# Scores of a 32-head attention as fp32 products over 16 rows, in four diagonal tiles of TensorE's array

## The reference, cut to what matters

```
x = hidden_states                       # (4, 512, 512) fp32: 2048 tokens of 512
q = (x @ wq.T + bq).reshape(B, S, 32, 16)        # 32 heads of 16
k = (x @ wk.T + bk).reshape(B, S, 32, 16)
v = (x @ wv.T + bv).reshape(B, S, 32, 16)
scores  = einsum('bshd,bstd->bsht', q, k) / 4    # per token: 32 x 32, heads against heads
context = einsum('bsht,bstd->bshd', softmax(scores), v)
x = layernorm(x + context)
dq1, dq2, dq3 = nf4_quant_dequant(w1), nf4_quant_dequant(w2), nf4_quant_dequant(w3)
x = layernorm(x + (silu(x @ dq1.T) * (x @ dq2.T)) @ dq3.T)       # hidden width 1376
```

## Time and profile before

| | |
|---|---|
| median of 3 runs | 787.29 us (787.03 to 789.25) |
| the profiled execution's own time | 788.01 us |
| its span in the profile | 786.2 us |
| busy share of the span | PE 93%, DVE 81%, ACT 62%, POOL 14% |
| mean granted clock of TensorE | 0.862 of full speed |

### The profile page before, as it was taken

The page is one execution under the profiler, slowest core; times in us unless marked ns, Lnnn a source line. Parts: engine busy times, 40 slices in busy tenths (PEclk is TensorE's granted clock), DMA queues, the critical chain, the costliest instruction groups (busy, mean ns, idle before and its releaser), DMA issues.

```text
span 786.2 us, 14305 instructions
## 1 busy us (share of the span) xinstructions
PE 732.7 (93%) x5688; PEld 625.5 (80%) x5688; DVE 633.4 (81%) x876; ACT 484.6 (62%) x650; POOL 106.8 (14%) x101
## 2 busy tenths in 40 slices
PE   4899999966999989999999999999999999999983
PEld 4778788856999989999888877887887788888761
DVE  2699999975888988988888899999977986554386
ACT  3588979773645636546853878877756775333134
POOL 2011012113101101111101121121201111000022
PEclk9999999995555655555799999999999999999995
DMA  9964455999797695995413371211514010330347
GB/s 219 223 182 146 134 166 167 250 305 271 166 261 189 184 283 134 269 216 202 163 26 122 120 230 54 81 39 31 173 59 155 1 61 21 134 119 13 121 147 160
DMA packets 89474, 117.89 MB, mean 150 GB/s; under 512 B 24768, under 2 KB 70848, under 8 KB 86496
## 3 DMA queue, kind: packets, MB, share of 16 engines
q1 hardware_dynamic: 88272, 114.88, 51.6%
q10 hardware_dynamic: 1136, 2.10, 1.2%
HBM read 76.42 MB, written 38.86 MB: 147 GB/s over the span
## 4 chain that ended last, share of the span: by engine, by line
PE 54%; DVE 18%; issue 11%; ACT 8%; DMA 4%; SPq 4%; POOL 1%; DVEq 0%; POOLq 0%; ACTq 0%
PE ps_p L1043 10%; DVE nf_acc L1166 8%; PE ps_s L947 7%; PE ps_s L945 7%; PE ps_s L946 7%; PE ps_p L945 5%; PE ps_p L947 5%; PE ps_p L946 5%; ACT nf_y L777 4%; PE ps_s L1030 3%; PE ps_t L968 2%; DMA qk_parts<-qk_p 2%; DVE part L1298 2%; DMA k_st<-qk_parts 1%; ACT part L852 1%
## 5 line engine op out<-in xcount | busy, mean ns | idle before, releaser
L1166 DVE SCALAR_TENSOR_TENSOR nf_acc<-nf_y,nf_acc 128x1024 f32<-128x1024 f32 (+4 forms) x266 | 298.5, 1122 | 37.6 <-ACT nf_y L777 28.3
L777 ACT ACTIVATE nf_y<-nf_w,bound_b 128x1024 f32<-128x1024 f32 (+4 forms) x285 | 288.9, 1047 | 9.7 <-DVE nf_acc L1162 3.4
L1043 PE MATMUL ps_p<-probT,v_bd 128*68 128x32 f32 x1024 | 125.7, 301 | 7.9 <-issue 7.9
L1043 PEld LDWEIGHTS ps_p<-probT,v_bd 128*68 128x68 f32 x1024 | 122.7, 211 | 9.4 <-issue 8.0
L945 PE MATMUL ps_p<-x_hl,w_hl 128*128 128x512 f32 x192 | 77.6, 404 | 6.1 <-DVE w_hl L1184 4.1
L695 POOL TENSOR_TENSOR nf_w<-nf_w,nf_rec 128x1024 f32<-128x1024 f32 (+4 forms) x19 | 39.5, 2080 | 320.1 <-DVE nf_rec L1150 320.1
L1325 DVE TENSOR_TENSOR silu<-silu,ps_s 128x512 f32<-128x512 f32 (+1 forms) x44 | 30.1, 684 | 61.5 <-PE ps_s L947 61.5
L927 ACT ACTIVATE hid_hl<-silu 128x512 fp32r<-128x512 f32 (+1 forms) x44 | 27.8, 632 | 77.6 <-DVE silu L1325 77.6
L947 PE MATMUL ps_p<-x_hl,w_hl 128*128 128x512 f32 x192 | 75.5, 393 | 0.0
L945 PE MATMUL ps_s<-x_hl,f_ha 128*128 128x512 f32 x192 | 75.4, 393 | 0.0
L946 PE MATMUL ps_p<-x_hl,w_hl 128*128 128x512 f32 x192 | 75.3, 392 | 0.0
(11 more groups left out here) (110 smaller groups left out, 1253.1 us busy)
## 6 DMA issues: line engine op xcount, KB each, us to landing
x_hl<-x_parts SPq DMA_DIRECT2D x10, 2048.0 KB, 8.5
qk_parts<-qk_p SPq DMA_DIRECT2D x64, 204.0 KB, 2.6
q_st<-qk_parts SPq DMA_DIRECT2D x48, 272.0 KB, 6.8
k_st<-qk_parts SPq DMA_DIRECT2D x48, 272.0 KB, 7.2
x_parts<-x_st SPq DMA_DIRECT2D x16, 512.0 KB, 4.4
nf_w<-in_L_ffn_w SPq DMA_DIRECT2D x24, 256.0 KB, 3.0
dequantised<-nf_acc SPq DMA_DIRECT2D x10, 512.0 KB, 2.6
v_blocks<-v_t SPq DMA_DIRECT2D x16, 256.0 KB, 3.5
```

The source lines that it names most:

```text
L777: act.activation(nf_y[0:p, at % NY, 0:w], nf_w[0:p, u % 2, 0:w], ACT.Identity, bias=bound_b[0:p, i:i + 1], scale=STEEP).then_inc(s_ny, 1)
L1043: t = pe.matmul(ps_p[0:MV, (G + 3) % NPV, i * H:(i + 1) * H], v_bd[hb % 2][:, :, g * GI + i], probT[:, G % 2, i], start=True, stop=True)
L1166: dve.scalar_tensor_tensor(out=acc, in0=y, scalar=float(NF4[i + 1]), in1=acc, op0=ALU.min, op1=ALU.max).then_inc(s_nacc, 1)
```

## The change

- **Scores.** q and k are no longer split. They are stored as fp32 and loaded into stacks of the same name with 16 rows in each quarter of the partitions (rows 32q to 32q+15), a quarter of the half block's tokens in each. A product has 16 rows, and its result goes to the quarter of the same number. There are still 64 products for each group, now fp32.
- **Parts.** `part_high`, `part_rest`, `part_middle` and `part_low` give way to one `queries_keys` on ACT. The values' bias moves from ACT to DVE (`value`).
- **Values.** The operands change places: `probT` (128x32) is stationary and `v_bd` (128x68) is moving; the 16 products of a group go to four quarters of the partitions. The result has tokens and heads in rows, so ACT copies it out (`evacuate`, 128x272), PE transposes it back (`back`, four transposes of 128x68), and `context` copies that as before. The rows of `v_bd`, `q_st` and `k_st` are padded from 64 to 68 elements (`VS`).
- **Transfers.** One store for each q or k product instead of two; eight loads for each pair of stacks instead of twelve, and no copies of zero rows. The stacks of half block 1, the values of 0 and the stacks of 0 are loaded in that order during the third and fourth block's projections (`FIRST_LOADS`). `clear(0)` is moved to the start.
- **Order.** `values(G-2)` is before the `ct` turns, `back(G-3)` behind them; contexts, `ct`, `moments`, `norm_1` and `xt` are all one step later, and two `xt` turns fall behind the last step. ACT works a step's levels ahead of its exponential. The levels are dealt out anew: 76 instead of 59 beside the projections, 45 instead of 55 beside the attention steps.
- **Rooms.** The feed-forward tensors lie in another order in SBUF.

```diff
-    Q_TERMS = (0, 1, 2, 0, 1, 0)
-    K_TERMS = (0, 0, 0, 1, 1, 2)
-    TS = TB + 16
+    VS = TI + 4
...
-    qk_d = nc.dram_tensor("qk_parts", [2, NHB, 3 * E, TS], BF16, kind="Internal").ap()
+    qk_d = nc.dram_tensor("queries_keys", [2, NHB, Q4, D, H, VS], F32, kind="Internal").ap()
...
+    FIRST_LOADS = {3 * KC * (NBK - 1) - 5: "stacks 1", 3 * KC * (NBK - 1) - 3: "values 0",
+                   3 * KC * (NBK - 1) + 1: "stacks 0"}
-    LV_P = [1, 1, 1, 1, 1, 1, 1, 1, 2, 2, 2, 2] * NBK
+    LV_P = [2, 1, 2, 1, 2, 1, 2, 1, 2, 2, 2, 2] + [2, 2, 1, 2, 2, 1, 2, 2, 1, 2, 1, 2] * (NBK - 1)
-    LV_A = [2] * GG
+    LV_A = [2, 1] * (GG // 2)
     for b in range(NBK - 1):
-        LV_A[8 * b + 10:8 * b + 13] = [1, 1, 1]
+        LV_A[8 * b + 11:8 * b + 14] = [1, 1, 1]
...
-        def load_stacks(eng, hb, which=range(3), sides=range(2)):
+        def load_stacks(eng, hb):
+            for i in range(2):
+                for q in range(Q4):
+                    eng.dma_start(stacks[hb % 2][i][32 * q:32 * q + D].rearrange("d h t -> d (h t)"),
+                                  qk_d[i, hb, q].rearrange("d h t -> d (h t)")).then_inc((s_ldq, s_ldk)[i][hb % 2], 16)
...
-            def part_high(n):
+            def queries_keys(n):
...
+                act.activation(qk_p[:, n % NQK, :, 0:TI], ps_p[:, tau % 3].rearrange("p (a t) -> p a t", t=TI),
+                               ACT.Identity, bias=bias[:, i, m:m + 1]).then_inc(s_qh, 1)
...
+            def evacuate(G):
+                act.wait_ge(s_pv, G + 1)
+                wait(act, s_back, G - NCT + 1)
+                act.activation(ctmp[:, G % NCT], ps_p[:, G % 2, 0:4 * MV], ACT.Copy).then_inc(s_evac, 1)
...
             for G in range(GG):
+                steep(LV_A[G])
                 for at in CONTEXT_AT.get(G, []):
                     context(at)
-                steep(LV_A[G] // 2)
                 exp(G)
+                if G >= 2:
+                    evacuate(G - 2)
...
                 for i in range(GI):
                     for q in range(Q4):
-                        s = q * TI + g * GI + i
+                        rows, s = slice(32 * q, 32 * q + D), g * GI + i
                         t = pe.matmul(ps_s[32 * q:32 * q + 32, G % 2, i * H:(i + 1) * H],
-                                      q_st[:, :, s], k_st[:, :, s], start=True, stop=True)
+                                      q_st[rows, :, s], k_st[rows, :, s], start=True, stop=True)
...
-                wait(pe, s_ctx, G - NPV + 1)
+                wait(pe, s_evac, G - 1)
                 for i in range(GI):
-                    t = pe.matmul(ps_p[0:MV, (G + 3) % NPV, i * H:(i + 1) * H], v_bd[hb % 2][:, :, g * GI + i],
-                                  probT[:, G % 2, i], start=True, stop=True)
+                    a, j = divmod(i, 4)
+                    t = pe.matmul(ps_p[32 * j:32 * j + 32, G % 2, a * MV:(a + 1) * MV], probT[:, G % 2, i],
+                                  v_bd[hb % 2][:, :, g * GI + i], start=True, stop=True)
                 t.then_inc(s_pv, 1)
+            def back(G):
+                pe.wait_ge(s_evac, G + 1)
+                wait(pe, s_ctx, G - 1)
+                for a in range(4):
+                    t = pe.transpose(ps_p[0:MV, 2 + G % 2, P * a:P * a + P], ctmp[:, G % NCT, a * MV:(a + 1) * MV],
+                                     ident[:])
+                t.then_inc(s_back, 1)
...
-            def part_rest(n):
...
-            def part_low(n):
...
+            def value(n):
...
+                dve.tensor_scalar(v_t[:, n % NV], ps_p[:, tau % 3], bias[:, 2, m:m + 1], None, ALU.add
+                                  ).then_inc(s_vev, 1)
```

More of the change, by code:

```diff
@@ L94, in layer_kernel, with pairs @@
     NU0 = len(GROUPS[0]) + 2
+    def pairs(g):
+        js, out = list(GROUPS[g]), []
+        while js:
+            n = 2 if len(js) > 1 and rows_of(js[1]) == P else 1
+            out.append(js[:n])
+            js = js[n:]
+        return out
     def turns_of(u):
         kind, g, _ = UNITS[u]
-        return [("f", u, s) for s in range(2 if kind == "w" else -(-len(GROUPS[g]) // 2))]
+        return [("f", u, s) for s in range(2 if kind == "w" else len(pairs(g)))]
     def valid(g):
@@ L312, in layer_kernel @@
         s_const = sem("s_const")
-        s_zero = sem("s_zero")
         s_vzero = [sem(f"s_vzero{i}") for i in range(2)]
-        s_szero = [sem(f"s_szero{i}") for i in range(2)]
         s_pad = sem("s_pad")
@@ L396, in parts_stored @@
             for r in range(NQK):
-                wait(eng, s_stq[r], 32 * of_slot(tiles, r, NQK))
+                wait(eng, s_stq[r], 16 * of_slot(tiles, r, NQK))
         def values_stored(eng, tiles):
@@ L733, in ones @@
                 pool.wait_ge(s_vzero[slot], 2 * Q4)
-            words = q_st1[:].rearrange("p h t -> p (h t)").bitcast(F32)
-            for q in range(Q4):
-                pool.memset(words[:, DV * TI * q:DV * TI * q + DV * TI], 0.0).then_inc(s_zero, 1)
             normalise(0)
+            clear(0)
+            ones(0)
             for tau in range(3 * KC * NBK):
-                if tau == VALUES_FREE + 2:
-                    clear(0)
-                    ones(0)
                 around(LV_P[tau])
@@ L902, in _ @@
                     norm_1(NORM_AT[G])
-                steep(LV_A[G] - LV_A[G] // 2)
+            context(GG - 4)
+            evacuate(GG - 2)
+            for key in XT_AT.get(GG, []) + TAIL_1:
+                high(key)
             context(GG - 3)
-            for key in TAIL_1:
-                high(key)
-            context(GG - 2)
             steep(LV_T[0])
@@ L910, in _ @@
                 high(key)
-            context(GG - 1)
+            evacuate(GG - 1)
+            context(GG - 2)
             steep(LV_T[1])
@@ L1104, in _ @@
                 scores(G)
+                if G >= 2:
+                    values(G - 2)
                 for key in CT_AT.get(G, []):
                     turn(key)
-                if G >= 2:
-                    values(G - 2)
+                for at in BACK_AT.get(G, []):
+                    back(at)
                 for key in XT_AT.get(G, []):
@@ L1111, in _ @@
             values(GG - 2)
-            for key in TAIL_1:
+            for key in XT_AT.get(GG, []) + TAIL_1:
                 turn(key)
+            back(GG - 3)
             values(GG - 1)
@@ L1116, in _ @@
                 turn(key)
+            back(GG - 2)
             pe.wait_ge(s_minus_i, 1)
@@ L1120, in _ @@
                 gate_up(s)
+                if s == 0:
+                    back(GG - 1)
                 for key in F_TURNS.get(s, []):
```

201 lines of the change are left out of this document (76 added, 125 removed).

## The result

The changed kernel takes 807.0 us (median of 4 runs, 802.5 to 809.3) against 788.3 for the kernel before in the same comparison: 1.024 times, with an interval of 1.021 to 1.027. It is slower; the forecast was 762, faster. The profiled execution took 808.4 us, span 806.6.

The account below looks back on a forecast made before the run. PE was taken to bind projections, feed-forward and about half the attention steps. Gains of 3.5 + 12.4 + 3.7 - 0.5 = 19.1 us took 788.0 to 768.9; half the clock's gain gave 762, range 740 to 792.

Parts of the forecast that it names:

- PE's step: Attention: PE's work per group falls from 5.15 to 4.41 us, scores 2.56, values 0.97, transposes back 0.88.
- the eight steps of 4.41 and the 144.4 us: Attention: eight opening steps take 35.3 us, 12.4 gained; steps from group 8 to 31 take 144.4, 3.7 gained.
- All this is worth nothing by itself: Projections: less DVE and ACT work gains nothing while PE is the bound; shorter PE waits gain 3.5 us.
- Opening: Start of attention: earlier clear and values' load remove the 7.91 us idleness; eight steps take 35.3 us, 12.4 gained.
- Tail: From group 31's maximum to the first feed-forward product: 16.1 us of PE work against 15.6, half a microsecond lost.
- Feed-forward: Feed-forward part: same matmuls, seven levels fewer beside them, no gain because PE covers DVE and ACT.
- Clock: Attention: TensorE's granted clock rises to between 0.6 and 0.8; full level worth 13.5 us, half taken, giving 761.5.
- dear products: Rival, attention: fp32 tiles overlap less, scores and values cost more; 811 us at two tiles, 790 to 835; chance 0.18.
- The late load: Rival, opening: SP falls behind with stores, values' load stays late, hole of some 8 us remains; 770 us; 0.17 with floor.
- The gain into idleness: Rival, attention: PE's gain goes only into idleness, at a step of 5.2 us; 782 us; chance 0.08.
- DVE alone binding: Rival, attention: scores near 1.3 us and clock up, PE leaves the chain; about 745 us, at best 738; chance 0.12.
- The floor between starts: Rival, scores: 25 ns a product record makes the step 5.05 us; 774 us; chance 0.17 together with late load.

Follow-up runs that it names:

- 100 pairs a step: Kernel before with only the values turned round and `v_bd` rows of 68 words: 789.2 us; the same without the later stacks' loads: 778.2 us.
- half the records: Changed kernel with score products reading only the upper bf16 half of each fp32 word, 64 records instead of 128: 774.8 us, 0.987 of the kernel before.

## Why the prediction was wrong, point by point

Three terms of the sum failed: the steps' time, which took PE's instructions as always there (13 us); the projections with the hand-over, where the new deal of levels was to cost nothing (14 us); and the tail with what follows, summed from PE's work alone (13 us).

**PE's step: right as work, wrong as time.** Forecast 2.56 + 0.97 + 0.88 = 4.41 us; measured as lengths of runs 2.14 to 2.50, 1.20 and 1.07, from start to start 4.39. The step that failed is the one from there to the eight steps of 4.41 and the 144.4 us: it priced records by their pace and took for granted that PE's instructions are there when wanted. The change raised them from 96 to 164 pairs a step and shortened the step in which they must arrive. The kernel before had 6.9 us of such gaps ahead of its scores, and the prediction passed over them; the 7.91 us in the earlier trace rows were the values' load, as it said. In their place stand 36.6 us of such gaps; that they cost the steps 13 us net of what hides behind them is the difference to the forecast, not a run of its own. Without the later loads the steps take 173.8 us, under the forecast's 179.7. That blocks of 256 instructions come late is read from the gaps' places and the packets' count, and borne out by the runs without later loads (21.8 of 36.6 us left; and 1.8 of 27.9 after 200 us at 100 pairs a step, without the stacks').

**"All this is worth nothing by itself" and +3.5 us for the projections: wrong, -5.6.** DVE's 119 us beside PE's 142.5 said that PE covers it. On average it does. But levels put into the first projections stand ahead of the splits that PE waits for (6.3 us in one wait), and the new deal brought first operations of units next to GpSimd's work: 3.35 us for one beside the clear of `v_bd_0`, 1.86 and 2.31 beside scalings, and 6.10 beside a scaling and the clear of `v_bd_1`, each 0.7 otherwise. The last is the hand-over. The old deal gives back 8.4 and 3.9 us there, 5.0 in the tail and 3.1 behind it, takes 9.5 in the steps, and leaves 10.5 at the end. With it the first scores come 2.8 us earlier than in the kernel before, close to the 3.5 forecast: the gain from the missing splits was there, and the deal spent it.

**Opening: the mechanism was right.** The hole before the first `values` is gone; 38.2 us from maximum 0 to 8 against 35.3 forecast and 47.7 before. The issue gaps took the rest.

**Tail: -8.9.** The forecast summed PE's work and left out DVE's and ACT's differences, ACT's wait for the stores and the order on SP. Under the old deal of levels it is 20.0 us, still 3.9 over the forecast; the change of SP's order turned one wait into another.

**Feed-forward: +3.8 us.** PE waited 5.2 us for `f_la` and `f_lb`, whose reloads came late. Under the old deal these waits are gone and 3.1 of the 3.8 us with them.

**Clock: right in size.** Granted 0.66 and 0.64, in the range given, against 0.57 and 0.54 before. What it gave back isn't shown by itself.

**The rivals.** Fp32 tiles overlap well: dear products, the one rival that ended slower, is refuted by the records; the time it gave (811) came out by another cause. The late load didn't come true. The gain into idleness (782) is near in kind: PE's busy time from 216 to 380 us fell by 34 us and the 31 steps by 3. DVE alone binding was seen only with half the records. The floor between starts: a score record takes 2.14 us / 128 = 17 ns. By the Trainium skill ("TensorE: Matmul & The Clock Gate", section "Wait — 56ns, not 53.3ns?") it would be about 25; the runs disagree.

By the padding rule that the prediction cited from the Trainium skill ("SBUF — State Buffer", section "Door 1: The DMA port swizzle") 64 and 68 words would be the same, both beyond its 16 bytes. The run of packed rows disagrees, 1.99 against 1.20 us; the measurement decides. The prediction also says that no row has a padded operand. That is wrong: the stacks of the kernel before have rows of 272 bf16 words for 256 tokens (`TS`), and their records take 20 ns, where those over the packed `v_bd` take 121.

## What to carry to other kernels

Count instructions as you count work: 128 pairs of load and multiply are one block to fetch, and such a block took 3.6 us at least (from gap to gap) and 7 to 8 us beside full DMA engines; what PE does faster than that it waits for. A row "issue" in the middle of a uniform run, at a multiple of 128 pairs, is that sign. And an engine that is busy less than the bound one isn't covered for every order of its work: ask what stands ahead of the first operation that the bound engine wants, and what the other engines do at that moment. Last, a wait's name isn't its cause: see what ended just before the wait did.

## What the runs showed of the hardware that was not expected

- Gaps in PE's work at multiples of 128 pairs, up to 4.6 us, 36.6 us in all; 21.8 without loads beside them. At 100 pairs a step: 39.4 with the DMA engines at 0.9 to 1.0 of their time, of these 27.9 after 200 us, and 1.8 there once the share is 0.4.
- With the moving operand's 68 elements 256 bytes apart, 32 records in four column quarters take 1.99 us, 272 bytes apart 1.20; and in the first case DVE's and ACT's 128x1088 operations beside them take 30% longer.
- DVE's `TENSOR_SCALAR` of 128x1024 or 128x1088 fp32, where it ran beside GpSimd's operations in the changed kernel, took 1.86 to 6.10 us instead of 0.7 (four cases): 3.35 with GpSimd's fill of 128x1156 words, x4, in 4.1 us beside it, 6.10 with a 2 us operation and that fill. The fill moved away, the 3.35 are 0.69 again.
